# First products of both MLPs in three float32r parts, their squares on ScalarE, and new instruction orders

## The reference, cut to what matters

```
def mlp(n, fc_w, proj_w):          # n: 256 x 128, fc_w: 128 x 512, proj_w: 512 x 128
    h = jax.nn.relu(n @ fc_w)
    return jnp.square(h) @ proj_w
```

## Time and profile before

| | |
|---|---|
| median of 3 runs | 925.98 us (922.77 to 926.07) |
| profiled execution | 926.01 us, its span 924.2 us |
| PE | 876.6 us busy, 95% |
| PEld | 754.2 us, 82% |
| DVE | 670.8 us, 73% |
| ACT | 550.5 us, 60% |
| POOL | 383.7 us, 42% |
| granted TensorE clock, mean | 0.993 |

### The profile page before, as it was taken

The page is one execution under the profiler, slowest core; times in us unless marked ns, Lnnn a source line. Parts: engine busy times, 40 slices in busy tenths (PEclk is TensorE's granted clock), DMA queues, the critical chain, the costliest instruction groups (busy, mean ns, idle before and its releaser), DMA issues. The chain is left out here.

```text
span 924.2 us, 24882 instructions
## 1 busy us (share of the span) xinstructions
PE 876.6 (95%) x9248; PEld 754.2 (82%) x9248; DVE 670.8 (73%) x1867; ACT 550.5 (60%) x1192; POOL 383.7 (42%) x643
## 2 busy tenths in 40 slices
PE   2799999999999999999999999999999999999986
PEld 2587778888878888988989797988888888978775
DVE  7979889786877776787868677777688676668330
ACT  4545565846565856647386564637555765676841
POOL 1672343443244535334362543326252424553532
PEclk9999999999999999999999999999999999999998
DMA  8200000000000000000000000000000000000000
GB/s 281 87 2 18 8 7 2 7 2 2 19 2 8 13 2 18 8 12 14 2 19 2 18 2 1 19 1 13 2 2 2 12 1 15 1 13 1 13 12 12
DMA packets 17927, 15.71 MB, mean 17 GB/s; under 512 B 2065, under 2 KB 15761, under 8 KB 17553
## 3 DMA queue, kind: packets, MB, share of 16 engines
q1 hardware_dynamic: 17808, 14.12, 4.8%
HBM read 12.02 MB, written 2.10 MB: 15 GB/s over the span
## 5 line engine op out<-in xcount | busy, mean ns | idle before, releaser
L1167 PE MATMUL pool<-gH,w_h_hi 128*128 128x256 f32 x512 | 150.2, 293 | 4.4 <-POOL gL L535 2.2
L1167 PE MATMUL pool<-gH,w_h_lo 128*128 128x256 f32 x512 | 144.9, 283 | 0.0
L1167 PE MATMUL pool<-gL,w_h_hi 128*128 128x256 f32 x512 | 144.8, 283 | 0.0
L1061 DVE TENSOR_REDUCE mneg<-pool 128x2 f32<-128x512 f32 (+1 forms) x192 | 119.9, 683 | 26.3 <-PE pool L1167 25.9
L711 ACT ACTIVATE PT<-pool 128x512 f32<-128x512 f32 x192 | 102.3, 603 | 28.7 <-PE pool L1167 28.4
L629 ACT ACTIVATE BC<-pool 128x512 f32<-128x512 f32 x128 | 75.3, 603 | 68.0 <-PE pool L1167 65.3
L948 DVE TENSOR_TENSOR M<-pool,LM 128x512 f32<-128x512 f32 x128 | 87.6, 685 | 36.5 <-PE pool L1167 35.9
L1167 PE MATMUL pool<-BC 64*128 64x256 f32 (+1 forms) x1024 | 108.0, 345 | 1.9 <-DVE M L949 1.2
L494 POOL TENSOR_SCALAR_AFFINE_SELECT PT<-PT 128x256 f32<-128x256 f32 (+1 forms) x192 | 89.3, 486 | 39.9 <-ACT PT L711 37.8
L1167 PEld LDWEIGHTS pool<-BC 64*128 64x128 f32 x1024 | 87.4, 189 | 21.0 <-issue 11.1
L1167 PEld LDWEIGHTS pool<-gH,w_h_hi 128*128 128x128 f32 x512 | 97.2, 190 | 8.2 <-issue 3.8
(11 more groups left out here) (233 smaller groups left out, 2361.1 us busy)
## 6 DMA issues: line engine op xcount, KB each, us to landing
X<-in_x SPq DMA_DIRECT2D x16, 128.0 KB, 2.1
...
```

The costliest lines, as they stand in the source:

```text
L1061: v.reduce_max(dst, o, axis=AX.X, negate=True).then_inc(S["mx"], 1)
L1167: return p.matmul(o, lhsT, rhs, start=start, stop=True, skip_group_check=True)
```

## The change

1. `w_mfc` and `w_afc` are split in two float32r parts at the start (`phi(3)`, `phi(4)` on ACT, `plo(3)`, `plo(4)` on DVE). The raw weights land in `gate` and in a half of `val`, so `ga(0)` waits for `plo(3)` and `conv(1, 0)` for `plo(4)`.
2. `t2c` and `t5c` write a high part (`t2H`, `t5H`). New DVE steps `t2l` and `t5l` write the low part from the bank. `up` and `upb` wait for those and issue `split_product`: 6 MATMULs for each step, for 4 before.
3. `sq` and `sqb` become ACT steps, Square in place on `hid`. The bank is given back by `relu` and `relub`.
4. To make room, `x2n` becomes `l1` and `ytm` a part of `yv`, and their waits follow (`ln1` waits for `t6` of the example before, `yv` for `t4` of the example before). `ident_bf` shrinks from 128 to 32 columns, filled by four copies. Two masks and one row of scales land in other tiles.
5. All five written orders and the bank list are new. PE's list has the same 976 steps. At the start it begins `tin gat inv bc bc bc bc cb cb` in place of `tin inv bc gat bc bc cb cb`. DVE's begins `dec st0 dec ag0 m01 dec xh dec xm dec dec st0 nrm ag0 plm st0 plm plm xh xm plo plm plm xnlo plo plo ag0 plo plo fold conv conv conv plm m conv plm plm m m nrm fold fold m m m xnlo m m conv`. Before it was `st0 dec ag0 m01 dec xh dec xm dec dec dec nrm plo plo plo st0 xnlo plm plm ag0 plm fold conv conv conv xh m plm conv st0 plm plm fold xm ag0 fold m plm plm nrm m m xh fold xnlo m m m m conv`. ACT's begins `pxx ss1 pex pex pex pex pex phi xnhi phi phi phi phi pex pex bcx`, before `pxx ss1 phi phi pex phi xnhi pex pex pex bcx`. Where PE's list ends, the steps of the last example stand in the same order as before; ACT has `relub relub sqb sqb` there.

```
-    t2=(1, "t2c"), up=(1, "sq"), ... t5=(1, "t5c"), upb=(1, "sqb"),
+    t2=(1, "t2l"), up=(1, "relu"), ... t5=(1, "t5l"), upb=(1, "relub"),
...
-    w_mfc, w_afc = sb("w_mfc", [P, HID]), sb("w_afc", [P, HID])
+    w_mfc, w_afc = split("w_mfc", HID), split("w_afc", HID)
...
@ scalar
+            elif k == 3:
+                act.wait_ge(in_c, 16 * 4)
+                a.activation(w_mfc[0][:], raw_mfc, ACT.Copy).then_inc(p_hi, 1)
+            elif k == 4:
+                act.wait_ge(in_d, 16 * 11)
+                a.activation(w_afc[0][:], raw_afc, ACT.Copy).then_inc(p_hi, 1)
...
-            a.activation(t2s[:], bank("t2", i)[:, 0:L], ACT.Copy).then_inc(S["t2c"], 1)
+            a.activation(t2H[:], bank("t2", i)[:, 0:L], ACT.Copy).then_inc(S["t2c"], 1)
...
+        def sq(i, k):
+            act.wait_ge(S["relu"], at("relu", i, k))
+            h = hid[:, 0, 2 * k:2 * k + 2, :]
+            a.activation(h, h, ACT.Square).then_inc(S["sq"], 1)
...
@ vector
+            elif k > 2:
+                w, raw = (w_mfc, raw_mfc) if k == 3 else (w_afc, raw_afc)
+                v.tensor_tensor(w[1][:], raw, w[0][:].bitcast(F32), ALU.subtract).then_inc(p_lo, 1)
...
+        def t2l(i, _):
+            dve.wait_ge(S["t2c"], at("t2c", i))
+            v.tensor_tensor(t2L[:], bank("t2", i)[:, 0:L], t2H[:].bitcast(F32), ALU.subtract).then_inc(S["t2l"], 1)
...
-        def sq(i, k):
-            dve.wait_ge(S["relu"], at("relu", i, k))
-            h = hid[:, 0, 2 * k:2 * k + 2, :]
-            v.scalar_tensor_tensor(h, halves(bank("up", i, k)), 0.0, h, ALU.max, ALU.mult).then_inc(S["sq"], 1)
...
@ tensor
         def up(i, k):
-            pe.wait_ge(S["t2c"], at("t2c", i))
+            if i == 0 and k == 0:
+                pe.wait_ge(p_lo, 4)
+            pe.wait_ge(S["t2l"], at("t2l", i))
             o, = claim("up", i, k)
             for b in range(2):
-                last = mm(o[:, b * L:(b + 1) * L], w_mfc[:, (2 * k + b) * P:(2 * k + b + 1) * P], t2s[:], b == 0)
+                last = split_product(o[:, b * L:(b + 1) * L], w_mfc, (2 * k + b) * P, t2H[:], t2L[:], b == 0)
             last.then_inc(S["up"], 1)
```

More of the change, by code:

```diff
@@ L32 @@
     yt=1, t4=1, o=1, t5=1, upb=2, downb=1, t6=1, w1=2, w2=2, h1=2, h2=2, w3=1,
-    ss1=1, xnhi=1, ga=1, val=1, xp=1, bcx=8, ss2=1, t2c=1, relu=2, ss3=1, t3c=1, qk=1, vv=1, qtc=2, ktc=1,
-    ex=12, yv=1, t4c=1, ss4=1, t5c=1, relub=2, t6hi=1, sl=2, ghi=2, ge1=2, hhi=2, ge2=2,
+    ss1=1, xnhi=1, ga=1, val=1, xp=1, bcx=8, ss2=1, t2c=1, t2l=1, relu=2, ss3=1, t3c=1, qk=1, vv=1, qtc=2, ktc=1,
+    ex=12, yv=1, t4c=1, ss4=1, t5c=1, t5l=1, relub=2, t6hi=1, sl=2, ghi=2, ge1=2, hhi=2, ge2=2,
     st0=1, ag0=1, xh=1, xm=1, nrm=1, xnlo=1, conv=4, m=8, yg=1, xm2=1, xa=1, e2=1, nw=14, rp=3, qs=2, mx=12, mh=2, qm=4, yn=2,
@@ L41 @@
     tin=(1, "xnlo"), inv=(1, "conv"), gat=(1, "ga"), vt=(1, "xp"), bc=(1, "bcx"), cb=(2, "m"), v=(1, "yg"), out=(1, "xm2"),
-    t2=(1, "t2c"), up=(1, "sq"), down=(1, "xa"), t3=(1, "t3c"), qkv=(1, "rp"), qt=(1, "qtc"), kt=(1, "ktc"), s=(4, "mx"),
-    mt=(1, "qm"), e=(4, "ex"), pv=(1, "yv"), yt=(1, "yn"), t4=(1, "t4c"), o=(1, "xa2"), t5=(1, "t5c"), upb=(1, "sqb"),
+    t2=(1, "t2l"), up=(1, "relu"), down=(1, "xa"), t3=(1, "t3c"), qkv=(1, "rp"), qt=(1, "qtc"), kt=(1, "ktc"), s=(4, "mx"),
+    mt=(1, "qm"), e=(4, "ex"), pv=(1, "yv"), yt=(1, "yn"), t4=(1, "t4c"), o=(1, "xa2"), t5=(1, "t5l"), upb=(1, "relub"),
     downb=(1, "xa3"), t6=(1, "t6lo"), w1=(1, "sl"), w2=(1, "gt"), h1=(1, "ge1"), h2=(1, "ge2"), w3=(1, "ln3"))
@@ L49 @@
     PE=(
[26 rows of a table removed]
[26 rows of a table added]
     ),
     Activation=(
-        "pxx ss1 phi phi pex phi xnhi pex pex pex bcx pex pex bcx bcx pex pex bcx val ga bcx ss1 xp bcx fhi bcx xnhi bcx fhi "
-        "fhi bcx fhi fhi bcx bcx bcx val bcx bcx xp ss2 bcx t2c fhi bcx relu relu ss1 ga fhi xnhi t3c ss3 qk vv bcx bcx ga "
-        "bcx t2c fhi fhi relu relu ss2 bcx bcx bcx val ss1 xp ss3 t3c qk ktc qtc qtc bcx bcx xnhi bcx bcx bcx ex ex ex ex ga "
[7 rows of a table removed]
-        "sl val sl ga relu t4c ghi bcx xp bcx bcx ghi ss1 t5c ss4 bcx ktc bcx qtc qtc ge1 ge1 hhi hhi relub relub ex ex ex ex "
[11 rows of a table removed]
@@ L100 @@
-        "ex ex bcx bcx bcx val yv vv t6hi xp bcx bcx sl sl ga qtc ktc qtc bcx bcx ghi ghi t4c bcx ss4 ge1 hhi ge1 t5c hhi ex "
[6 rows of a table removed]
+        "pxx ss1 pex pex pex pex pex phi xnhi phi phi phi phi pex pex bcx bcx pex bcx ss1 bcx ga bcx val bcx xp bcx bcx xnhi "
+        "fhi fhi fhi fhi fhi bcx bcx val bcx bcx bcx xp fhi fhi t2c ss2 bcx bcx bcx relu relu ss1 sq sq xnhi t3c ss3 ga qk "
+        "bcx bcx vv bcx t2c ss2 relu relu ss1 sq sq bcx bcx val ga bcx xp fhi t3c ss3 qk qtc ktc qtc bcx bcx xnhi bcx bcx bcx "
@@ new lines @@
+        "ex ex ex ex ga val ss2 t2c xp ex ex ex ex relu ss1 bcx bcx fhi relu ex ex ex ex bcx vv yv bcx bcx fhi sq sq t4c xnhi "
+        "ktc t5c qtc qtc ga val bcx bcx relub ss2 relub t2c bcx sqb bcx bcx sqb ss1 ss4 xp bcx bcx bcx ss3 ex t3c ex ex t6hi "
[13 rows of a table added]
+        "vv bcx bcx t2c bcx ghi relu sq relu ss2 ss4 t5c ga ge1 ss1 ge1 sq hhi ktc hhi qtc relub relub bcx bcx qtc val sqb "
[3 rows of a table added]
+        "ss4 bcx t6hi xp bcx bcx bcx sl sl ghi ghi t5c ss1 qtc ktc ge1 relub hhi ge1 hhi qtc relub sqb sqb sq sq ge2 ge2 ss2 "
[8 rows of a table added]
@@ L107 @@
     ),
     DVE=(
-        "st0 dec ag0 m01 dec xh dec xm dec dec dec nrm plo plo plo st0 xnlo plm plm ag0 plm fold conv conv conv xh m plm conv "
[36 rows of a table removed]
+        "dec st0 dec ag0 m01 dec xh dec xm dec dec st0 nrm ag0 plm st0 plm plm xh xm plo plm plm xnlo plo plo ag0 plo plo "
[35 rows of a table added]
     ),
     Pool=(
-        "zero r1 r1 r2 r2 r1 r1 r1 r2 r2 r1 xr fsc fsc fsc fsc flo fsc fsc flo fsc gp fsc fsc flo fsc xr flo xr flo flo zero "
[3 rows of a table removed]
-        "r8 r8 sel r4 r4 sel sel sel sel sel sel sel outp glo glo hlo hlo r8 r8 r5 r5 gp sel sel sel r1 sel r6 r6 x1 sel xr "
@@ L165 @@
-        "sel hlo hlo sel sel sel sel r7 r4 r4 r7 sel sel sel sel r8 r8 glo glo hlo hlo r5 r5 outp sel sel sel sel sel r6 r6 "
-        "sel x1 sel sel r7 r7 sel sel sel sel r8 r8 glo glo hlo outp r5 r5 hlo r6 r6 x1 r7 r7 glo glo hlo hlo r8 r8 outp r8 "
+        "zero r1 r1 r2 r2 r1 r1 r2 xr r2 r1 r1 fsc fsc fsc fsc flo flo flo fsc fsc gp fsc flo flo fsc xr fsc flo xr fsc zero "
+        "r2 r3 r2 r3 xr gp r1 r1 r4 r4 xr xr xr r1 r1 r2 r2 r3 r3 gp sel sel flo sel sel xr r1 xr xr sel r1 sel sel sel r2 r4 "
@@ new lines @@
+        "r2 r4 r3 sel sel sel sel gp xr r3 xr r3 flo flo flo r5 r2 r5 r6 r6 r1 x1 r7 r7 sel r1 xr r3 sel sel sel r2 gp sel "
+        "sel sel sel glo glo sel sel r4 sel sel r4 hlo r3 xr hlo xr r5 r5 r6 r6 x1 r2 r2 r7 r7 sel sel sel sel r8 r8 sel sel "
+        "sel sel r1 sel outp sel r4 sel r4 sel glo glo hlo hlo r8 r8 r3 r5 r5 gp sel sel sel sel r6 r6 x1 xr xr sel r1 r7 sel "
[7 rows of a table added]
+        "outp sel sel sel sel glo glo gp r1 hlo hlo r5 gp r8 xr sel xr sel sel sel xr r8 sel sel r3 sel sel xr r2 r5 sel r2 "
@@ new lines @@
+        "sel sel sel outp r6 r6 r3 x1 xr r4 r4 r7 r7 r5 glo glo r1 r3 hlo hlo r5 r2 r2 r1 gp xr xr r6 r6 r3 xr r8 r8 sel sel "
+        "sel sel x1 sel sel sel sel r4 r7 r7 sel r3 sel r4 sel sel glo glo r2 r2 r3 gp hlo hlo sel sel xr r5 r5 sel outp xr "
+        "sel sel sel sel r6 r6 x1 r4 sel r7 r7 xr r4 sel sel sel sel r3 r3 r5 r5 gp sel sel sel sel glo glo sel sel sel sel "
+        "r6 r6 r8 r8 sel sel outp r4 sel xr r3 r4 sel xr x1 hlo hlo r7 r7 r8 r8 r5 glo glo xr r5 outp r6 r6 r3 sel sel x1 sel "
@@ L167 @@
+        "sel hlo hlo r7 r7 sel sel sel sel r4 r4 sel sel sel sel r8 r8 glo glo r5 outp hlo hlo sel sel sel sel r5 sel r6 r6 "
+        "x1 sel sel sel r7 r7 sel sel sel sel glo glo r8 r8 r5 r5 outp hlo hlo r6 r6 x1 r7 r7 r8 r8 glo glo outp hlo hlo r8 "
         "r8 outp"
@@ new lines @@
+    "6521376521316721501356701234567670231456020374512074501264536745637561243756431275623514761415672350671234524014"
+    "6724167245473016750123560123456701231345672341567243154236745123674503465710242657165235176257605236745023012314"
+    "0416753206275324067104567034534675034016734013457013701274572340123567023670152326746470142367401236071423160236"
+    "7014232670124506714203563175460705314565701234567014560712340561234501276450126745301267450124567671245124502340"
+    "1250126701234567014014567423501674052367104102367142351607235601235623015650123450352032067014532673014536017260"
@@ L190 @@
+    "1672045671204567120206714353675231645237016270450123670123456764017234560172362014523601621453260145603271401202"
+    "5634715230674512674537452367234670614501672305167213053670123567015236754012367540120364750167213245671234567341"
+    "0516102134501672450124675201467250146201567014635376014357601755012301012301246750123467153204671026537451026373"
+    "45102562013401034567102354671023540761230354761235470654231212130101001023401010"
 )
@@ L258, in program @@
```

(66 more changed lines are left out.)

57 lines of the change are left out of this document (21 added, 36 removed), and 185 rows, old and new, of tables (Activation, DVE, PE, Pool).

## The result

The changed kernel takes 915.9 us (913.82 to 916.95, four runs), against 925.18 us for the kernel before on the same chip, also four runs. The ratio is 0.9909, interval 0.9885 to 0.9933. I had forecast 917.5 us, in a range of 910 to 926. The profiled span is 914.9 us, 9.3 less than before.

A forecast was written before the change was run, and what follows sets the result against it. PE was taken to bound the middle (99% busy), VectorE to pace the start, a chain through one example the end. 926.0 - 9.9 (products) + 0.8 (borders) + 0 (start) + 0 (middle) + 0.6 (end) = 917.5 us, range 910 to 926.

The forecast's parts named there:

- PE's product term: In `up` and `upb`, three float32r matmuls replace two float32 ones, 0.077 us cheaper per product; 128 products give -9.9 us.
- borders: On PE, entering float32r groups from other work costs 0.10 us each; 22 more entries, some others gone, net +0.8 us.
- The start: First large product 5 us later, given back by the last `m(0, 7)` as DVE's work sum counts; 0 us, -2 to +5.
- The middle: From 100 to 870 us, added ACT and DVE steps cost nothing beside PE's 99%; 0 us, -2 to +6.
- The end: Behind the last `upb`, ACT's `relub(1)` and two squares take 1.9 us before `downb`, where PE idled 1.41; +0.6 us.
- ACT and DVE: Busy times: squares move from DVE to ACT, DVE to about 642 us, ACT near 595, table loads 73 to 75.
- the first: Squares on ACT's list stand in front of what PE waits for; slower than 930.6 us, up to 958; chance 0.09.
- The second: Freed time not kept: start's 5 us stay (922.5, chance 0.09) or middle's DVE and POOL chains take back nine (926.5, 0.08).
- The third: A float32r matmul costs a quarter of a float32 product in the new places: -13.9, 913.5 us; chance 0.08.
- The fourth: New orders also close 5 us or more of PE's gaps at start and end: 912 us or less; chance 0.06.

The follow-up runs named there:

- up_one_f32: The changed kernel with one float32 product of the high parts in `up` and `upb` in place of three float32r ones; 923.1 us, ratio 0.9987 to the kernel before.
- start_early: The changed kernel with `fold(1)`, `fold(2)` right behind `fold(0)`, and `phi(0)`, `plo(0)`, `xnhi(0)`, `xnlo(0)` ahead of the decay tables; 904.61 us.
- before_folds_late: The kernel before with `fold(0, 1)` and `fold(0, 2)` moved on DVE's list to right behind the second `nrm`; 930.06 us, ratio 1.0053.
- folds-early kernel: The changed kernel with `fold(1)` and `fold(2)` moved on DVE's list to right behind `fold(0)`; 905.69 us, ratio 0.9796 to the kernel before.

## Why the prediction was right

The number was 1.6 us off, and that is in part luck: the layout (-5 to -7 us) and PE's shorter list (some -7) were in no term, and the folds (+10) took most of both away again. Term by term:

1. **PE's product term** (-9.9, and +0.8 for borders): measured -7.2 us of time, -8.3 of PE's busy time. Right in kind; right in size within the intervals, whose half width is 1 to 2 us for each of the two times. The MATMUL count is right. The distance of 0.1185 on which I built it was itself a property of the layout: with the 0.1157 of the changed kernel the sum is 128 x (0.432 - 0.347) = -10.9, and +1.6 for 16 more entries into float32r groups than in up_one_f32, so -9.3. PE's busy time shows one microsecond less than that.
2. **What I did not have: the layout.** 64 bytes between run-time tiles and weights give -5.4 (put into the kernel before) or -6.7 us (taken out of the changed one). Everything on the earlier trace rows ran at 0.1185 and I took that as the price of the instruction. Half of the unexpected fall of PE's busy time is this.
3. **The start, "0 us".** This is the step that failed, and its range (+5) was too narrow. Both halves of the argument have to be told apart. That a late `inv(0)` and `gat(0)` are made up for is borne out: start_early moves them forward by 3.5 us and keeps at most one. That what DVE must do until the last `m(0, 7)` keeps its length was wrong. I counted instructions at the durations that they have in the old place; the folds had an idle GpSimd beside them there, and in the new place they last 11.7 us. It cost 10.2 us, in the traces 8.7 of PE's idle time and 1.7 of its busy time, with the granted clock at 0.95 behind the wait. The last `m` of example 0 ended at 54.3 us, not near 47. The 1.77 us that I took off for the fourth `fold` had the same fault: the same instruction takes 0.68 in before_folds_late, where GpSimd is idle.
4. **The middle, "0 us" (-2 to +6).** Idle time rose by 2.4 us, inside the range. The reason I gave, that the squares have cover because neither engine is near PE's share, is not enough: in the old order they cost 14 us, with ACT at 62% and DVE at 67% of the span. What covers them is where they and their neighbours stand in the lists.
5. **The end, +0.6:** the idle time before `downb` is 1.93 us for 1.41, +0.5.
6. **ACT and DVE:** 73 table loads became 75, as counted. ACT is busy 586.6 us, 36.1 more than before, where I had 595; the 64 squares make 38.2 of it at 0.62 to 0.63 each. DVE is busy 659.1, where I had about 642. With the folds early it is 649.3, so 10 of the 17 us too many are the folds; the other 7 are not traced.

The sum in two steps that have the same MATMULs and the same distance: from the kernel before with 64 bytes ahead (span 919.9, PE 871.0) to the changed kernel with float32 products (923.1, 866.1) everything else together, orders and squares and moved tiles, costs +3.2 us of span (+3.8 by the medians). Inside it are the +10 of the folds, so the rest of the new order brings about -7. The folds-early kernel has as little idle time as the kernel before (48.4 and 47.6), so those -7 are busy time of PE, not closed gaps: 866.1 for 871.0, which is -4.9, and 1.7 more that the late folds hide.

Adding up the distances from each MATMUL to the next by tiles shows part of it: the transposes take 66.6 to 67.1 us in the eight traces with the old order of PE and 64.6 to 65.3 in the six with the new one, `cb` takes 102.1 to 104.3 and 99.6 to 102.0, and the float32 `up` and `upb` 57.8 to 58.2 in the old order and 56.3 in the new (up_one_f32). I cannot say which neighbours in PE's new list save it; I counted only the borders of float32r groups. This stays open. The whole: -4.3 (layout) + 3.2 - 8.2 (products) = -9.3 us of span. Each of these is a difference of single profiled executions and good to some 2 us.

The rivals: the first was real but had been covered by the orders. The second (the start's 5 us stay) had the right place and sign and the wrong cause. The third, in which the one pass for a float32r matmul was a conclusion of mine, is out by up_one_f32. The fourth did not happen.

A rule of the Trainium skill bears on the folds. "SBUF — State Buffer", section "SBUF: two separate sides", says that VectorE shares one pair of SBUF ports with GpSimd by an exclusive lock, held for a whole instruction, and that a VectorE instruction takes it in a 2-port mode or when it reads two SBUF inputs while GpSimd reads SBUF too; the loser stands still. I did not bring it to bear on the moved folds. The trace agrees: 1.23 to 1.35 us for casts that take 0.18 to 0.29 alone, 1.35 for 0.29 and 1.75 for 0.68 us for two instructions with two inputs in SBUF, and 0.68 us unchanged for `m`, one of whose inputs is in PSUM. That it is this port and not another shared part, no run here shows.
